# Random-feature attention on TensorE: key and query features as pairs of 64-row products, context product with its sides exchanged

## The chip, the cores and the metric

The kernel runs on one core of one Trainium2 chip. The metric is device time in microseconds from one launch. Five engines work side by side: TensorE (PE, with its weight loads as PEld), VectorE (DVE), ScalarE (ACT), GpSimd (POOL) and SyncE (SP), which issues most DMAs. TensorE reads on-chip memory (SBUF) and writes the eight PSUM banks of 128 partitions by 512 float32. All data here is float32, and each float32 product of the source becomes two weight loads and two passes on TensorE (a transpose is one of each).

## The reference, cut to what matters

The program is a layer of a network on 1250 nodes of width 512. It adds a graph convolution with two relations (two rounds), an attention block of depth 2, and a product-key memory with gathered rows. The change lies in the attention block. With 8 heads of 64 and 256 random features, each of its two layers computes (g and b left out):

```
def softmax_kernel(data, proj, is_query, eps=0.0001):
    normalizer = d ** (-0.25)
    data_dash = einsum('bhnd,md->bhnm', data * normalizer, proj)
    diag = sum(data ** 2, -1, keepdims=True) * 0.5 * normalizer ** 2
    m = max over features (query) or over nodes and features (key)
    return ratio * (exp(data_dash - diag - m) + eps)
q, k, v = y @ Wq + bq, y @ Wk + bk, y @ Wv + bv        # 8 heads of 64
qp, kp = softmax_kernel(q, proj, True), softmax_kernel(k, proj, False)
ctx = einsum('bhnm,bhnd->bhmd', kp, v);  k_sum = kp.sum(nodes)
o = einsum('bhmd,bhnm,bhn->bhnd', ctx, qp, 1 / (qp @ k_sum))
x = x + o @ Wo + bo;  then layer norm, MLP with gelu
```

## The kernel before, in words

The 1250 nodes are 10 tiles of 125 (`P`); the q, k, v products work on 5 pairs of tiles (`PAIRS`). There are no tiles chosen by a planner: each engine has its own hand-written list of instructions, in order, and semaphores in `m[...]` join them. `l` is the attention layer. Layer 0 runs from about 28 us to 380 us, then the MLP (to 668 us) and the two rounds of the graph convolution (to 1263 us), then attention layer 1 (to 1598 us), then the memory, with the MLP of layer 1 in it, to the end.

**Projection.** `projbd` (128 x 512) is a block-diagonal matrix: rows 0 to 63 hold the scaled projection in columns 0 to 255, rows 64 to 127 in columns 256 to 511, and the rest is zero. One product of k or q (128 rows = two heads) with it gives the features of two heads, 512 columns, in one bank. `attn1_dve` makes it at lines 460 to 464 by two zeroings and two scaled copies, ahead of the first norm (L483).

**Keys (`attn1_*`).** For each pair of tiles i, PE does the products for q, k, v (L570, L577, L584), the sums of squares in four 32-column groups (L590), and then 8 units n (tile j = n // 4, two heads c = n % 4), each one product at L610 into bank 4 + n % 4. Before unit 2 stand four transposes of the sums (L605), before unit 4 the 8 transposes of the next pair's normed rows (`turn(i + 1)`, L559). DVE takes the maximum of each unit (L514), ACT then copies the unit to `kdash` (L642), and this frees the bank: unit n waits for the copy of unit n - 4. DVE after unit 1: `spread` (L489) and the next norm (L483), for which `turn` waits. ACT after the copy of unit 3: `scale(i + 1)` (L623), for which the next q products wait. In layer 0 DVE has other work in its list too: 160 comparisons for the graph's edges (L356), 32 of them among the units of the first pair, the others among the k products, and the edge indices (L364 to L372), after unit 3 in pairs 1 to 4. A short chain of small steps over DVE and PE (L524 to L533) then forms the shift over all keys.

**Context (`attn2_*`).** ACT takes the exponentials (L656), DVE adds eps (L668), and PE multiplies for 10 tiles and 8 heads (L678): stationary `v_aug` (125 x 65: values and a column of ones), moving `kdash` (125 x 256), result 65 x 512 for two heads in one of banks 0 to 3. DVE and ACT copy these to `ctx_t` (L671, L661); in `attn3_pe` 16 transposes (L805) and four more copies (L723, L758) bring them to `ctx_sb`, 128 features by 65.

**Queries (`attn3_*`).** 40 units n (tile T, two heads c) go through a software pipeline on all three engines. In step n PE does the feature product of unit n (L800, banks 6, 7, 0, 1), the four transposes of unit n - 2 (L818), and the four output products of unit n - 3 (L829, 8 passes with 125 x 65); once per four steps also `out_turn` (L784) and `out_mm` (L792, 8 passes of 512 columns). DVE in step n: maximum (L715), bias (L717), copy with eps of unit n - 2 (L727), every second step a normalisation (L700, L702), every fourth, where n % 4 is 2, the residual (L707, L709) for n from 10. ACT: two exponentials (L749), and the copy L762. The transposes of units u with u % 4 = 1 write the bank that the residual reads, so they wait for L707 (line 814). SP's loads of the MLP's weights wait for `ctx`, and the loads of the graph's bases (L439) for the last residual. POOL scatters the edges in layer 0 (L284) in its own time, and then adds the two copies of the adjacency by DMA (L291).

## Time and profile before

| | us |
|---|---|
| median of 3 runs | 2761.16 |
| lowest, highest | 2752.94, 2769.96 |
| profiled execution, span from first to last instruction | 2754.8 |
| profiled execution, own time beyond its span | not given |
| PE busy | 2409.9 |
| DVE busy | 1468.9 |
| ACT busy | 681.1 |
| POOL busy | 1036.3 |

"Busy" is the time in which an engine executes; a PE product's end is modelled and lies some 0.16 us behind the start of the next, so the distance between starts is the better measure of its price. All steps below are taken from the profiled execution; L numbers are lines of the kernel.

### The profile page before, as it was taken

The numbers are of one execution on the slowest core, as the hardware profiler recorded it, in microseconds if no ns is written. First come the engines' busy times: TensorE is split into PE (matmuls) and PEld (weight loads), VectorE is DVE, ScalarE is ACT, GpSimd is POOL, SyncE is SP. The second block draws the span as 40 slices with busy tenths as digits, with TensorE's granted clock in tenths as the row PEclk, the third lists the DMA queues.
The fourth block names the chain that finished last, engine by engine and source line by source line (L and its number), as shares of the span: only waits on it lengthen the run. The fifth ranks groups of instructions, "written<-read, shape, count | busy, mean of one in ns | idle before, by whom it ended". The sixth has DMA issues, their size and how long they took to land.

```text
span 2754.8 us, 27581 instructions
## 1 busy us (share of the span) xinstructions
PE 2409.9 (87%) x9500; PEld 1234.4 (45%) x9500; DVE 1468.9 (53%) x3793; ACT 681.1 (25%) x1687; POOL 1036.3 (38%) x885
## 2 busy tenths in 40 slices
PE   3999989997999999999999987889879879875665
PEld 2656656665444444445656654433333333331210
DVE  3765675455666300002345614477677677677664
ACT  1346231211110011002364211223322332321222
POOL 0066877760111000000000000566666656666665
PEclk9999999998999999999999998999999999987856
DMA  9934145478466601440005000799999989989998
GB/s 304 297 64 127 2 109 117 98 157 223 160 181 196 154 1 52 108 112 19 1 1 172 1 8 8 267 327 342 337 327 342 335 316 348 333 317 340 341 358 313
DMA packets 235969, 524.42 MB, mean 190 GB/s; under 512 B 99362, under 2 KB 99737, under 8 KB 231675
## 3 DMA queue, kind: packets, MB, share of 16 engines
q0 software_dynamic: 170032, 379.99, 42.2%
q1 hardware_dynamic: 57477, 137.07, 16.2%
q10 hardware_dynamic: 8330, 5.71, 0.7%
q8 instruction: 71, 1.16, 0.2%
q14 instruction: 59, 0.48, 0.1%
HBM read 489.51 MB, written 45.34 MB: 194 GB/s over the span
## 4 chain that ended last, share of the span: by engine, by line
PE 67%; DVE 13%; DMA 8%; issue 5%; POOL 3%; another core or an unknown queue 2%; ACT 1%; SPq 0%; DVEq 0%; POOLq 0%; ACTq 0%
PE bank L1070 12%; PE bank L1325 6%; PE bank L1047 5%; PE bank L905 4%; PE bank L916 4%; PE bank L1305 4%; PE bank L1315 3%; PE bank L1259 3%; PE bank L678 3%; PE bank L792 3%; PE bank L570 3%; PE bank L584 2%; PE bank L1057 2%; PE bank L577 2%; DMA qv<-in_L_ffn_rows,qv 2%
## 5 line engine op out<-in xcount | busy, mean ns | idle before, releaser
L1228 POOL DMA_INDIRECT qv<-in_L_ffn_rows,qv x356 | 360.1, 1012 | 1009.4 <-issue 909.0
L1448 ACT ACTIVATE stage<-stage,qv 128x32 f32<-128x32 f32 x640 | 200.3, 321 | 576.8 <-issue 199.0
L1325 PE MATMUL bank<-qv,stage 128*32 128x512 f32 x712 | 257.6, 699 | 91.6 <-ACT stage L1448 48.4
L1612 DVE SCALAR_TENSOR_TENSOR qv<-qv,wreg 128x512 f32<-128x512 f32 x356 | 262.8, 746 | 118.2 <-DMA qv<-in_L_ffn_rows,qv 98.0
L284 POOL DMA_INDIRECT adj<-e_cnt,e_idx x80 | 163.7, 2046 | 193.7 <-issue 176.4
L284 POOL DMA_INDIRECT adj_b<-e_cnt,e_idx x80 | 167.3, 2091 | 62.5 <-issue 35.3
L1305 PE MATMUL bank<-stage,big 128*128 128x250 f32 x640 | 174.2, 399 | 7.5 <-ACT stage L1407 7.5
L1228 POOL DMA_INDIRECT big<-in_L_ffn_rows,qv x142 | 145.8, 1027 | 88.1 <-PE bank L1325 40.5
L1315 PE MATMUL bank<-big 128*125 128x512 f32 x320 | 173.0, 633 | 2.1 <-issue 2.1
L1070 PE MATMUL bank<-big,wreg 125*125 125x512 f32 x400 | 172.0, 592 | 0.0
L1070 PE MATMUL bank<-big,qv 125*125 125x512 f32 x400 | 171.8, 592 | 0.0
L1325 PE MATMUL bank<-big,stage 128*32 128x512 f32 x284 | 135.1, 722 | 35.9 <-ACT stage L1448 21.0
L1305 PEld LDWEIGHTS bank<-stage,big 128*128 128x128 f32 x640 | 115.6, 194 | 108.0 <-issue 91.1
L878 DVE SCALAR_TENSOR_TENSOR qv<-wreg,att_b,qv 128x2048 f32<-128x2048 f32 x60 | 138.4, 2348 | 32.9 <-DMA wreg<-in_L_gnn_basis 30.3
L1047 PE MATMUL bank<-qv,stage 128*125 128x512 f32 x320 | 148.1, 607 | 0.0
L1131 DVE TENSOR_TENSOR big<-bank,big 125x512 f32<-125x512 f32 x20 | 13.8, 692 | 247.2 <-PE bank L1070 247.2
L905 PE MATMUL bank<-stage,big 128*128 128x250 f32 x640 | 138.8, 377 | 1.2 <-ACT stage L937 1.2
L916 PE MATMUL bank<-big 128*125 128x512 f32 x320 | 139.0, 592 | 0.0
L1612 DVE SCALAR_TENSOR_TENSOR big<-big,qv,wreg 128x512 f32<-128x512 f32 x142 | 105.4, 746 | 55.0 <-DMA big<-in_L_ffn_rows,qv 48.9
L905 PEld LDWEIGHTS bank<-stage,big 128*128 128x128 f32 x640 | 122.4, 192 | 20.1 <-issue 6.0
L1325 PEld LDWEIGHTS bank<-qv,stage 128*32 128x32 f32 x712 | 32.2, 115 | 213.3 <-ACT stage L1448 109.8
L1099 POOL DMA_DIRECT2D stage<-in_L_gnn_basis x45 | 35.8, 955 | 226.1 <-DVE qv L1111 226.1
(227 smaller groups left out, 3984.8 us busy)
## 6 DMA issues: line engine op xcount, KB each, us to landing
wreg<-in_L_gnn_basis SPq DMA_DIRECT2D x30, 1024.0 KB
stage<-in_L_gnn_basis POOLq DMA_DIRECT2D x45, 512.0 KB, 4.5
big<-in_L_mix_W SPq DMA_DIRECT2D x4, 4096.0 KB
adj<-adj_b POOLq DMA_DIRECT2D x9, 1328.1 KB, 37.5
adj<-wreg SPq DMA_DIRECT2D x5, 2187.5 KB
adj_b<-wreg SPq DMA_DIRECT2D x5, 2187.5 KB
wreg<-adj SPq DMA_DIRECT2D x10, 1093.8 KB
qv<-adj SPq DMA_DIRECT2D x10, 1093.8 KB
```

Of the source, the lines that this page charges most:

```text
L284: nc.gpsimd.indirect_dma_start(out=(adj, adj_b)[g % 2], out_offset=bass.IndirectOffsetOnAxis(ap=e_idx[:, g:g + 1], axis=0), in_=e_cnt[:, g ...
L878: nc.vector.scalar_tensor_tensor(wrel[:, 0, r, :], wreg[:, n % BRING, :], att_b[:, 0, ds(i * BLOCKS + (r * BASES + n), 1)], wrel[:, 0, r, ...
L905: mm = nc.tensor.matmul(psum[F1_BANKS[n % 4]][:, 0:PT], w1_sb[:, k, 128 * n:128 * n + 128], y_t[:, k, :], start=(k == 0), stop=(k == KC - 1))
L916: mm = nc.tensor.matmul(psum[5 + j][0:P, :], act_t[:, k % HH, P * j:P * j + P], w2_sb[:, k, :], start=(k == 0), stop=(k == HC - 1))
L1047: mm = nc.tensor.matmul(psum[2 + 3 * j + r][0:P, :], gx_t[:, j, P * k:P * k + P], wrel[:, gl, r, 512 * k:512 * k + 512], start=(k == 0), s ...
L1070: mm = nc.tensor.matmul(psum[AGG_BANKS[j]][0:P, :], slabs[gl][:, j, c, :], zrel[:, c, :], start=(c == 0), stop=(c == COLT - 1))
L1228: nc.gpsimd.indirect_dma_start(out=ring[place(t, s)], out_offset=None, in_=a["L0_ffn_rows"], in_offset=bass.IndirectOffsetOnAxis(ap=slots_ ...
L1305: mm = nc.tensor.matmul(psum[F_BANKS[n % 2]][:, 0:PT], w1_sb[:, k, 128 * n:128 * n + 128], y_t[:, k, :], start=(k == 0), stop=(k == KC - 1))
L1315: mm = nc.tensor.matmul(psum[5 + j][0:P, :], act_t[:, k % HH, P * j:P * j + P], w2_sb[:, k, :], start=(k == 0), stop=(k == HC - 1))
L1325: nc.tensor.matmul(psum[7][WIDE * g:WIDE * g + WIDE, :], wsel[:, s % DRING, :], ring[place(t, s)][:, DIM:ROW], start=(s < 4), stop=(s >= S ...
L1448: nc.scalar.activation(wsel[:, s % DRING, :], mask, ACT.Relu, scale=inner[:, s:s + 1]).then_inc(p_diag, 1)
L1612: nc.vector.scalar_tensor_tensor(ring[place(t, s)][:, 0:DIM], ring[place(t, s)][:, 0:DIM], probs_of[t % 2][:, s:s + 1], xrep[:, s % 4, :], ...
```

## The change

The projection is kept once, as 128 rows by 256 columns (both halves alike). A step with two units n and n + 1 now does four products of 64 rows and 256 columns: heads in rows 0 to 63 (s = 0) go to one bank, heads in rows 64 to 127 (s = 1) to the next. So the units of a pair come from the same two 128-row blocks, and each bank holds the two heads of one s. Waits cover both banks. In the context product `kdash` is stationary (125 x 128, two halves per head) and `v_aug` moving (65 columns), which writes the layout of `ctx_sb` at once; `ctx_t`, its transposes and second copies are gone. `heads_of` picks the heads of a unit in the small tables of maxima and sums.

```diff
+        proj_t = projbd[:, 0:FEATS]
...
+        def heads_of(ap, u, s):
+            return ap.rearrange("p (u e s) -> p u e s", u=2, e=2)[:, u, :, s]
+        def two(ap):
+            return ap.rearrange("p (e m) -> p e m", e=2)
@@ -457,11 +464,7 @@
 
         def attn1_dve(dve, l):
             dve.wait_ge(m["pjT"], l * ADDS["pjT"] + 1)
-            for s in range(2):
-                rows = slice(64 * s, 64 * s + 64)
-                nc.vector.memset(projbd[rows, FEATS * (1 - s):FEATS * (2 - s)], 0.0).then_inc(m["pjS"], 1)
-                nc.vector.tensor_scalar(projbd[rows, FEATS * s:FEATS * s + FEATS], psum[7][rows, 0:FEATS], NORM, None,
-                                        ALU.mult).then_inc(m["pjS"], 1)
+            nc.vector.tensor_scalar(proj_t, psum[7][:, 0:FEATS], NORM, None, ALU.mult).then_inc(m["pjS"], 1)
             if l == 1:
                 dve.wait_ge(g_sem[1]["z"], 2 * TILES)
             else:
...
                     norm1(2 * i + 3)
                 for n in range(8):
-                    j, c = n // 4, n % 4
+                    j, u, s = n // 4, n % 4 // 2, n % 2
                     if l == 0 and i == 0 and n < 7:
                         merge_dve(dve, i, 4 * n + 4 * (n > 0), 4 + 4 * (n == 0))
                     dve.wait_ge(m["kd_pe"], l * ADDS["kd_pe"] + i * 8 + n + 1)
-                    nc.vector.tensor_reduce(kmax[:, 2 * i + j, 2 * c:2 * c + 2], psum[KD_BANKS[n % 4]][0:P, :].rearrange("p (s m) -> p s m", s=2),
+                    nc.vector.tensor_reduce(heads_of(kmax[:, 2 * i + j, :], u, s), two(psum[KD_BANKS[n % 4]][0:P, :]),
                                             AX, ALU.max).then_inc(m["kmx"], 1)
                     if n == 1:
...
                         mm = nc.tensor.matmul(psum[0][32 * c:32 * c + 32, PT * s:PT * s + PT], headsel[:, :], sq[:, s, c, :], start=True, stop=True,
                                               skip_group_check=True)
                 mm.then_inc(m["dg_mm"], 1)
-                for n in range(8):
-                    j, c = n // 4, n % 4
-                    if n < 2:
-                        pe.wait_ge(m["k"], l * ADDS["k"] + i * KC + KC + 1 + n)
-                    elif n < 4:
-                        pe.wait_ge(m["v"], l * ADDS["v"] + i * 2 + n - 1)
+                for n in range(0, 8, 2):
+                    j, u = n // 4, n % 4 // 2
+                    if n == 0:
+                        pe.wait_ge(m["k"], l * ADDS["k"] + i * KC + KC + 2)
+                    elif n == 2:
+                        pe.wait_ge(m["v"], l * ADDS["v"] + i * 2 + 2)
                     else:
-                        pe.wait_ge(m["kd"], l * ADDS["kd"] + i * 8 + n + 1)
+                        pe.wait_ge(m["kd"], l * ADDS["kd"] + i * 8 + n + 2)
...
                         turn(i + 1)
-                    nc.tensor.matmul(psum[KD_BANKS[n % 4]][0:P, :], k_t[:, c, P * j:P * j + P], projbd[:, :], start=True, stop=True).then_inc(m["kd_pe"], 1)
+                    for e in range(2):
+                        for s in range(2):
+                            rows = slice(64 * s, 64 * s + 64)
+                            mm = nc.tensor.matmul(psum[KD_BANKS[n % 4 + s]][0:P, FEATS * e:FEATS * e + FEATS], k_t[rows, 2 * u + e, P * j:P * j + P], proj_t[rows, :],
+                                                  start=True, stop=True, skip_group_check=True)
+                            if e == 1:
+                                mm.then_inc(m["kd_pe"], 1)
 
             pe.wait_ge(m["gmx"], l * ADDS["gmx"] + 1)
...
                 for n in range(8):
-                    j, c = n // 4, n % 4
+                    j, u, s = n // 4, n % 4 // 2, n % 2
                     if l == 1 and i == 2 and n == 0:
                         act.wait_ge(g_sem[1]["st"], 16 * PAIRS)
                     act.wait_ge(m["kmx"], l * ADDS["kmx"] + i * 8 + n + 1)
-                    nc.scalar.activation(kdash[:, 2 * i + j, 512 * c:512 * c + 512], psum[KD_BANKS[n % 4]][0:P, :],
-                                         ACT.Copy).then_inc(m["kd"], 1)
+                    nc.scalar.activation(kdash[:, 2 * i + j, :].rearrange("p (u e s m) -> p u e s m", u=2, e=2, s=2)[:, u, :, s, :],
+                                         two(psum[KD_BANKS[n % 4]][0:P, :]), ACT.Copy).then_inc(m["kd"], 1)
                     if n == 3 and i < PAIRS - 1:
                         scale(i + 1)
 
 
...
                         op.then_inc(m["kx"], 1)
+            if l == 0:
+                act.wait_ge(s_idx, 4 * PAIRS)
             for b in (1, 3):
                 act.wait_ge(m["ctx_pe"], l * ADDS["ctx_pe"] + b + 1)
-                nc.scalar.activation(ctx_t[:, 512 * b:512 * b + 512], psum[b][0:HD + 1, :], ACT.Copy).then_inc(m["cTa"], 1)
+                to, got = context_out(b)
+                nc.scalar.activation(to, got, ACT.Copy).then_inc(m["ctx"], 1)
 
         def attn2_dve(dve, l):
             for t in range(TILES):
@@ -668,16 +681,18 @@
                     nc.vector.tensor_scalar(kt, kt, EPS_K, None, ALU.add).then_inc(m["kf"], 1)
             for b in (0, 2):
                 dve.wait_ge(m["ctx_pe"], l * ADDS["ctx_pe"] + b + 1)
-                nc.vector.tensor_copy(ctx_t[:, 512 * b:512 * b + 512], psum[b][0:HD + 1, :]).then_inc(m["cT"], 1)
+                to, got = context_out(b)
+                nc.vector.tensor_copy(to, got).then_inc(m["ctx"], 1)
 
         def attn2_pe(pe, l):
             for t in range(TILES):
                 for hh in range(HEADS):
                     if hh % 4 == 0:
                         pe.wait_ge(m["kf"], l * ADDS["kf"] + 2 * t + hh // 4 + 1)
-                    mm = nc.tensor.matmul(psum[hh // 2][0:HD + 1, FEATS * (hh % 2):FEATS * (hh % 2) + FEATS],
-                                          v_aug[:, t, hh, :], kdash[:, t, FEATS * hh:FEATS * hh + FEATS],
-                                          start=(t == 0 and hh % 2 == 0), stop=(t == TILES - 1), skip_group_check=True)
+                    for q in range(2):
+                        mm = nc.tensor.matmul(psum[hh // 2][:, (HD + 1) * (2 * (hh % 2) + q):(HD + 1) * (2 * (hh % 2) + q + 1)],
+                                              kdash[:, t, FEATS * hh + 128 * q:FEATS * hh + 128 * q + 128], v_aug[:, t, hh, :],
+                                              start=(t == 0 and hh % 2 == 0 and q == 0), stop=(t == TILES - 1), skip_group_check=True)
                     if t == TILES - 1 and hh % 2:
                         mm.then_inc(m["ctx_pe"], 1)
...
                     dve.wait_ge(m["qd_pe"], l * ADDS["qd_pe"] + n + 1)
-                    nc.vector.tensor_reduce(qmax[:, n % 4, :], psum[QD_BANKS[n % 4]][0:P, :].rearrange("p (s m) -> p s m", s=2), AX, ALU.max).then_inc(m["qm"], 1)
+                    nc.vector.tensor_reduce(qmax[:, n % 4, :], two(psum[QD_BANKS[n % 4]][0:P, :]), AX, ALU.max).then_inc(m["qm"], 1)
                     dve.wait_ge(m["qm"], l * ADDS["qm"] + n + 1)
-                    nc.vector.scalar_tensor_tensor(qneg[:, n % 4, :], qmax[:, n % 4, :], -1.0, diag[:, T, 0, 2 * c:2 * c + 2],
+                    nc.vector.scalar_tensor_tensor(qneg[:, n % 4, :], qmax[:, n % 4, :], -1.0, heads_of(diag[:, T, 0, :], c // 2, c % 2),
                                                    ALU.mult, ALU.subtract).then_inc(m["qn"], 1)
-                if n == 1:
-                    for b in (0, 2):
-                        dve.wait_ge(m["cT_pe"], l * ADDS["cT_pe"] + b + 1)
-                        to, got = context_out(b)
-                        nc.vector.tensor_copy(to, got).then_inc(m["ctx"], 1)
                 if 2 <= n < UNITS + 2:
                     u = n - 2
                     dve.wait_ge(m["qT_pe"], l * ADDS["qT_pe"] + u + 5)
...
                     op.then_inc(m["qx"], 1)
-                if n == 1:
-                    if l == 0:
-                        act.wait_ge(s_idx, 4 * PAIRS)
-                    for b in (1, 3):
-                        act.wait_ge(m["cT_pe"], l * ADDS["cT_pe"] + b + 1)
-                        to, got = context_out(b)
...
             for n in range(UNITS + 6):
-                if n < UNITS:
-                    T, c = n // KC, n % KC
-                    pe.wait_ge(m["qx"], l * ADDS["qx"] + n + 1)
-                    nc.tensor.matmul(psum[QD_BANKS[n % 4]][0:P, :], q_t[:, c, P * T:P * T + P], projbd[:, :], start=True, stop=True).then_inc(m["qd_pe"], 1)
-                if n == 1:
-                    for b in range(4):
-                        pe.wait_ge(m["cTa" if b % 2 else "cT"], l * ADDS["cT"] + b // 2 + 1)
-                        for u in range(4):
-                            mm = nc.tensor.transpose(psum[T_BANKS[b]][:, (HD + 1) * u:(HD + 1) * (u + 1)], ctx_t[:, 512 * b + 128 * u:512 * b + 128 * u + 128],
-                                                     ident[0:HD + 1, 0:HD + 1])
-                        mm.then_inc(m["cT_pe"], 1)
+                if n == 2:
+                    pe.wait_ge(m["ctx"], l * ADDS["ctx"] + 4)
+                if n < UNITS and n % 2 == 0:
+                    T, u = n // KC, n % KC // 2
+                    pe.wait_ge(m["qx"], l * ADDS["qx"] + n + 2)
+                    for e in range(2):
+                        for s in range(2):
+                            rows = slice(64 * s, 64 * s + 64)
+                            mm = nc.tensor.matmul(psum[QD_BANKS[n % 4 + s]][0:P, FEATS * e:FEATS * e + FEATS], q_t[rows, 2 * u + e, P * T:P * T + P], proj_t[rows, :],
+                                                  start=True, stop=True, skip_group_check=True)
+                            if e == 1:
+                                mm.then_inc(m["qd_pe"], 1)
                 if 2 <= n < UNITS + 2:
                     u = n - 2
-                    if u < 2:
-                        pe.wait_ge(m["ctx"], l * ADDS["ctx"] + 4)
                     pe.wait_ge(m["qx"], l * ADDS["qx"] + u + 5)
                     if u % KC == 1 and u >= 9:
...
                         pe.wait_ge(m["o"], l * ADDS["o"] + 2 * T + 1 + c // 2)
-                    for s in range(2):
-                        hh = 2 * c + s
+                    for e in range(2):
+                        hh = 4 * (c // 2) + 2 * e + c % 2
                         for q in range(2):
                             mm = nc.tensor.matmul(psum[4 + hh // 4][0:P, (HD + 1) * (hh % 4):(HD + 1) * (hh % 4 + 1)],
-                                                  qfeat_t[:, v % 2, P * (2 * s + q):P * (2 * s + q) + P], ctx_sb[:, 2 * hh + q, :],
+                                                  qfeat_t[:, v % 2, P * (2 * e + q):P * (2 * e + q) + P], ctx_sb[:, 2 * hh + q, :],
                                                   start=(q == 0), stop=(q == 1), skip_group_check=True)
                     if c % 2:
                         mm.then_inc(m["o_pe"], 1)
```

## Rows read from the trace of the kernel before

**Rows 1.** The page: busy time by engine
```profile
PE 2409.9 (87%) x9500; PEld 1234.4 (45%) x9500; DVE 1468.9 (53%) x3793; ACT 681.1 (25%) x1687; POOL 1036.3 (38%) x885
```

**Rows 2.** Stretches: length; PE, PEld, DVE, ACT, POOL busy; PE clock; DMA share; GB/s
```profile
1425.30:1461.40 36.10, 36.09 (x161) 22.88 (x162) 14.56 (x21) 30.15 (x76) 0.00 (x0) 0.96 0.00 1
1479.00:1584.00 105.00, 99.77 (x537) 65.45 (x535) 67.22 (x157) 30.63 (x72) 0.00 (x0) 1.00 0.22 68
```

**Rows 3.** Groups by line: context product, maximum of the query features
```profile
L678 PE MATMUL bank<-big,qv 125*65 125x256 f32 x320 | 73.7, 395 | 6.0 <-DVE big L668 6.0
...
L715 DVE TENSOR_REDUCE small<-bank 125x2 f32<-125x512 f32 x80 | 55.1, 689 | 79.6 <-PE bank L800 79.0
```

**Rows 4.** Timeline of PE in the memory stage: a product of 64-row pairs
```profile
1990.66 0.80 PE L1305 MATMUL bank<-stage,big 128*128 128x250 f32 x3
1991.39 0.70 PE L1273 MATMUL bank<-wreg,qv 64*125 64x256 f32 x4
1992.02 0.69 PE L1315 MATMUL bank<-big 128*125 128x512 f32 x1
```

**Rows 5.** Timeline of the key units of one pair, layer 1
```profile
1293.46 1.98 PE L610 MATMUL bank<-projbd,stage 128*125 128x512 f32 x4
...
1294.62 0.69 DVE L514 TENSOR_REDUCE small<-bank 125x2 f32<-125x512 f32 x1 [0.89 <-PE bank L610]
...
1295.35 0.60 ACT L642 ACTIVATE big<-bank 125x512 f32<-125x512 f32 x1 [1.16 <-DVE small L514]
...
1296.25 0.54 DVE L483 TENSOR_SCALAR stage<-h,mv,rs 125x512 f32<-125x512 f32 x1
...
1298.85 1.90 ACT L623 ACTIVATE stage<-bank,cols 128x250 f32<-128x250 f32 x4
...
1301.72 1.85 PE L570 MATMUL bank<-stage,wreg 128*128 128x250 f32 x8
```

**Rows 6.** Timeline of one query step with n % 4 = 2, layer 1
```profile
1511.70 1.02 PE L800 MATMUL bank<-projbd,qv 128*125 128x512 f32 x2
...
1512.56 0.59 PE L818 MATMUL bank<-ident,big 125*128 125x125 f32 x4
...
1512.76 0.69 DVE L715 TENSOR_REDUCE small<-bank 125x2 f32<-125x512 f32 x1 [4.04 <-PE bank L800]
1512.89 0.95 PEld L829 LDWEIGHTS bank<-ctx_flat,stage 128*125 128x125 f32 x8
1512.99 0.99 PE L829 MATMUL bank<-ctx_flat,stage 128*125 128x65 f32 x8
...
1513.81 1.07 PE L800 MATMUL bank<-projbd,qv 128*125 128x512 f32 x2
...
1514.70 0.68 DVE L707 TENSOR_TENSOR h<-bank,h 125x512 f32<-125x512 f32 x1
...
1515.53 0.62 PE L818 MATMUL bank<-ident,big 125*128 125x125 f32 x4 [0.64 <-DVE h L707]
```

**Rows 7.** Timeline from the last context pass to the first query transposes, layer 0
```profile
241.55 1.88 PE L800 MATMUL bank<-projbd,qv 128*125 128x512 f32 x4
...
243.27 1.02 PEld L805 LDWEIGHTS bank<-ident,stage 65*128 65x128 f32 x15 [0.29 <-issue]
...
245.83 0.65 PE L818 MATMUL bank<-ident,big 125*128 125x125 f32 x4 [0.50 <-ACT ctx_flat L758]
```

**Rows 8.** Timeline of DVE at the start of layer 1
```profile
1263.90 0.27 DVE L462 MEMSET projbd<- 64x256 f32 x1
...
1265.41 0.46 DVE L483 TENSOR_SCALAR stage<-h,mv,rs 125x512 f32<-125x512 f32 x1
```

**Rows 9.** Busy time and clock by stretch (columns as in rows 2), end of layer 0
```profile
370.20:373.60 3.40, 1.73 (x13) 1.26 (x11) 2.15 (x5) 0.21 (x1) 3.10 (x2) 1.00 0.23 1
373.60:377.00 3.40, 2.97 (x4) 1.41 (x5) 0.63 (x2) 3.40 (x2) 2.79 (x3) 0.50 0.16 3
```

**Rows 10.** Chain of work that ended last, between the MLP and the graph convolution
```profile
629.56 39.30 DMA wreg<-in_L_gnn_basis
```

13 lines of the change are left out of this document (5 added, 8 removed).

## Prediction

> **What bounds the kernel now.** I read the page first, then busy time by stretch, groups by line, and the timeline of each part that the change touches. The page gives PE 87% of the span and no other engine more than 53% [rows 1]. In layer 1 PE is busy for 36.09 of 36.1 us in the context product and for 99.77 of 105 us in the queries [rows 2]; DVE waits 79.0 us for the query product [rows 3]. So PE sets the pace, and a shorter PE list pays only as far as the other engines' chains let it. Two of these are near. In the query steps with n % 4 = 2 PE already idles 0.64 us for the residual L707 [rows 6]. In the key part the next q products need `scale(i + 1)`, which ends at 1298.85 + 1.90 = 1300.75, only 0.97 us ahead of their start at 1301.72 [rows 5].
>
> **Price of the products.** Before, a unit of 512 columns takes 1512.56 - 1511.70 = 0.86 us, two passes of 0.43 [rows 6]. Right after an output product it takes 0.05 more (1.07 against 1.02, rows 6), because 65 columns don't cover the next weight load. The new form has a near relative in the memory stage [rows 4]: three passes of 250 columns, 0.21 each, end at 1990.66 + 0.64 = 1991.30; the 64-row block is recorded from 1991.39; the next 128-row product is recorded at 1992.02, with 0.69 instead of the usual 0.59 us, so its columns flow from 1992.12. Four passes of 256 columns thus cost 0.82 us: 0.43 for two streams side by side, and 0.39 for leaving and entering the 128-row form (0.09 of draining and 0.10 of bare weight load, twice). A new block has eight passes: 4 x 0.213 + 0.39 = 1.24 us for two units that cost 1.72 (1.82 behind output products). Two blocks in a row pay the switch once.
>
> The Trainium skill ("TensorEngine Tiling (Array Packing)", Key Properties) says that changing the tiling mode drains the engine. That speaks against this change: all query blocks stand alone between 128-row work. By that rule no block is free of the switch; the trace agrees and prices it at the 0.39 just read.
>
> **Projection.** Two zeroings and two copies run from 1263.90 until the norm at 1265.41, for which PE waits [rows 8]. One copy remains, about 0.4 plus 0.1 of hand-over; 1.0 us goes. In layer 0 the same four stand in the same DVE chain. Together -2.0.
>
> **Keys.** Zero is the record of the first unit, 1293.46 [rows 5]. New times: block 0 streams 0.10 to 0.96. DVE needs 0.20 more (rows 6: units end 1512.56, L715 starts 1512.76) and 0.69 per maximum, 0.61 back to back: unit 0 1.16 to 1.85, unit 1 to 2.46. ACT copies unit 1 to 3.09 (0.03 behind it, 0.60 long). The norm starts 0.08 behind unit 1's maximum (1294.62 + 0.86 + 0.69 = 1296.17 against 1296.25) and ends at 3.08. PE has done the four transposes of the sums and block 2 by 2.64, and must wait for this norm: a new stall of 0.6. `turn` 3.21 to 4.07, block 4 to 5.12, block 6 to 5.97. DVE takes units 2 and 3 to 4.30, ACT copies unit 3 until 4.93, `scale` (1.90) ends at 6.73, and q flows at 6.92. PE's list alone would be ready at 6.17; before it was 8.26. So 1.34 us per pair instead of 2.1: the wait that is late next is ACT's `scale`. The last pair has neither `turn` nor `scale`; its last maximum starts 1.0 earlier by the same count. Layer 1: 4 x 1.34 + 1.0 = 6.4. In layer 0 the first pair's units are paced by DVE with its edge comparisons, gain 0; three pairs 4.0; the last 0.5, since the edge indices stand in DVE's list before its last four maxima. Keys together -10.9.
>
> **Context.** 160 passes of 256 columns per layer, by columns half of 0.43, 0.2145 each, 34.3 us (the group's 73.7 us for both layers hold some half clock, rows 3). They become 320 passes with 128-column loads and 65 moving columns. The trace has this kind nearly: the output product's eight loads of 125 columns start over 0.95 - 0.19 = 0.76 us, 0.109 apart [rows 6], twice what 65 columns would stream. For 128 columns I take 0.112: 35.7 us, a loss of 1.4 per layer, +2.8. From below, the transposes' 128-column loads come (1.02 - 0.14) / 14 = 0.063 apart [rows 7]; that would be 20.1 us, a gain of 14 per layer. I stay at 0.112, because the 0.109 row is also a two-pass product. ACT with 30.15 us of work in this stretch [rows 2] keeps up.
>
> The Trainium skill ("TensorE: Matmul & The Clock Gate", Weight-path perf modes) says that fast weight load is not used for FP32 operands. By this the 0.063 is out of reach for a product and the 0.109 row is the right one; the transposes' row shows that some float32 loads do run faster.
>
> **Edits at nothing.** The maxima, copies and biases keep their sizes and only step over other heads; the wait for both banks is in the times above; ACT's moved wait for the edge indices in layer 0 is met long before the context ends. The MLP's weight loads start with `ctx`, some 2 us earlier, and nothing reads them for over 100 us.
>
> **Turn-around.** From the last context pass to the first query transposes it is 245.83 - 241.55 = 4.28 us, ended by the second copies L758 [rows 7]. New: switch and block 0 to 1.05, block 2 to 1.90 (the direct copies are ready before), maximum 1.25 to 1.94, bias, two exponentials (0.85), transposes at 3.1. Half a microsecond of later waits on unit 1 is made up by the unit that PE is ahead. -1.5 per layer, -3.0.
>
> **Queries.** Units 4 to 9: two units cost 2 x (0.91 + 0.43 + 0.82) = 4.32 before [rows 6], 3.74 after for n % 4 = 2; for n = 4 another 0.4 is lost waiting for L727. With 0.5 at n = 8 this is 1.3. From n = 10, steps with n % 4 = 2: zero is 1511.70; before, the transposes wait until 3.83 [rows 6]. The wait hangs on the first unit's maximum, which started at 1.06 and now starts at 1.25; so they start at 4.04, PE idle 1.5 instead of 0.86 (the second unit no longer fills this gap), and the half period is 0.2 longer. The other half (block, two times transposes and output product, `out_turn`, `out_mm`) is bound by PE and saves 1.77 - 1.24 = 0.53. Net 0.33 in each of 7 periods, -0.2 for the last: 2.1. Queries together -(1.3 + 2.1) x 2 = -6.8.
>
> **Sum.** -2.0 - 10.9 + 2.8 - 3.0 - 6.8 = -19.9 us, on the span of 2754.8: 2734.9. The median of the runs lies 6.4 above that span, within their spread, so I forecast 2761.2 - 19.9 = 2741.3. This asks that layer 0's share (9.3) comes through the MLP: there the last loads of the bases, 39.30 us on the chain [rows 10], share the DMAs with POOL's adding of the adjacencies. They start when DVE frees a buffer, so I let them move with it.
>
> **Rivals.**
> A, the chains give way (ACT's `scale` or the residual come earlier than I count) and PE's list decides. All of it would be 2.1 for each of 10 key pairs, 21 against my 10.9, and 0.53 for each of 36 query blocks, 19 against 6.8: 22 more, 2719. Half of it, which is what I mean by A: 2730. For it: PE's share [rows 1]; against it: the idle time already in rows 6 and the small slack in rows 5.
> B, slower: the clock falls in the context product. Its passes would stream 0.054 of every 0.112 us for 36 us on end. At the end of layer 0 PE is busy 1.73 of 3.4 us, and the next stretch has 0.50 of the full clock, 1.2 instead of 2.4 GHz; four passes of 512 columns fill 2.97 us there, not 4 x 0.43 [rows 9]. At that level a context pass costs twice, up to 36 us more per layer: 2741 + 72 = 2813. Against it: there PE also stood idle, here it never does. From about 20 us at half clock on, it outweighs the whole gain.
> C, the two row halves don't overlap, since a block has four products over two banks where rows 4 has two. A block then costs 0.85 more. By PE's list a key pair takes 1.3 more than before (nine pairs, 12), the second half of a query period 0.3 more (5), the first half 0.6 more by the later maximum (10); the other terms cancel: 2761 + 27 = 2788.
> D, layer 0's share is lost because the bases' loads end at a fixed time, set by the adjacency traffic: 2751.
>
> **Chances.** Forecast (2733 to 2749) 0.58, A 0.16, B 0.09, C 0.07, D 0.10. The range is 2720 to 2768; beyond it lie B and C, the far end of A and a fast weight load. A measurement of this kernel tells about 1% (27.6 us) from no change. Faster by more (below 2733.6) takes A or the low edge of the forecast: 0.27. Slower by more is B and half of C: 0.12. Within: 0.61.
>
> **What would show it.** Right: L610 and L800 blocks whose four passes of one row half come 0.21 apart with a partner beside each; L559 waiting 0.6 for L483 in the key part; the first L570 of a pair 6.9 us behind the first unit, ended by ACT L623; L678's successor with starts 0.11 apart and the stretch near 37 us; L818 waiting 1.5 for L707. Wrong: passes of a block one after the other (C), a clock below 0.9 in the context stretch (B), no wait of L559 (A), an MLP that ends earlier while the graph convolution doesn't (D).

## The result, and the profile after

The changed kernel takes 2828.45 us (median of 4 runs, 2809.09 to 2835.95), the kernel before 2761.32 beside it: ratio 1.023, interval 1.019 to 1.027. It is slower by 67 us, where 20 us of gain were forecast. The profiled execution has a span of 2834.1.

Busy time and clock by stretch, kernel before. The bounds are the starts of the stages' first PE instructions: keys of layer 0, its global maximum of the keys, context product, queries, then the MLP, then the four parts of layer 1, then the memory stage. The graph convolution and two parts of layer 1 are left out here (`...`; the two are shown with E5 and in rows 2). Columns as in rows 2.

```profile
28.40:200.00 171.60, 152.85 (x623) 100.29 (x623) 107.21 (x488) 60.92 (x126) 37.26 (x19) 1.00 0.75 231
200.00:204.20 4.20, 0.62 (x3) 0.34 (x3) 1.60 (x5) 2.66 (x8) 3.33 (x3) 0.85 0.20 1
204.20:241.60 37.40, 37.35 (x161) 23.43 (x162) 15.41 (x21) 30.18 (x76) 31.08 (x16) 0.93 0.17 2
241.60:387.10 145.50, 129.71 (x698) 84.95 (x696) 92.67 (x223) 46.99 (x95) 106.11 (x54) 0.98 0.35 72
387.10:681.70 294.60, 280.03 (x1001) 187.27 (x1001) 161.25 (x98) 52.05 (x104) 165.59 (x85) 0.97 0.67 157
...
1263.30:1421.00 157.70, 152.23 (x622) 100.59 (x622) 51.55 (x97) 59.57 (x125) 0.00 (x0) 0.98 0.01 4
...
1461.40:1599.10 137.70, 128.26 (x697) 84.35 (x695) 86.98 (x202) 39.99 (x93) 0.00 (x0) 1.00 0.26 87
1599.10:2754.80 1155.70, 911.40 (x4016) 362.30 (x4016) 738.65 (x2390) 312.65 (x900) 650.19 (x640) 0.88 0.82 296
```

The same view of the changed kernel:

```profile
28.20:195.00 166.80, 144.16 (x703) 102.26 (x703) 104.42 (x486) 60.32 (x126) 21.84 (x11) 0.98 0.76 237
195.00:199.70 4.70, 0.61 (x3) 0.33 (x3) 2.09 (x5) 3.16 (x9) 4.03 (x3) 0.69 0.18 1
199.70:268.20 68.50, 68.48 (x322) 68.36 (x322) 14.90 (x21) 29.46 (x74) 56.35 (x29) 0.50 0.18 2
268.20:428.60 160.40, 138.70 (x762) 101.98 (x761) 92.80 (x220) 46.84 (x93) 119.26 (x61) 0.84 0.33 64
428.60:714.50 285.90, 280.06 (x1000) 187.27 (x1001) 159.16 (x94) 52.14 (x104) 143.01 (x73) 0.98 0.66 162
...
1295.40:1445.50 150.10, 140.51 (x702) 100.11 (x702) 48.10 (x94) 58.68 (x125) 0.00 (x0) 0.98 0.01 4
1445.50:1450.00 4.50, 0.85 (x3) 0.57 (x3) 1.60 (x5) 4.04 (x9) 0.00 (x0) 0.56 0.00 0
1450.00:1518.50 68.50, 68.48 (x322) 68.36 (x322) 14.04 (x21) 29.94 (x76) 0.00 (x0) 0.50 0.00 1
1518.50:1668.30 149.80, 133.54 (x762) 98.06 (x762) 87.17 (x199) 39.77 (x91) 0.00 (x0) 0.88 0.24 80
1668.30:2834.10 1165.80, 919.54 (x4016) 366.44 (x4016) 738.97 (x2390) 313.31 (x900) 646.59 (x640) 0.87 0.81 293
```

The keys became shorter (171.6 to 166.8, 157.7 to 150.1). The context product became 31.1 and 32.4 us longer [rows 2 for layer 1 before], at a granted clock of 0.50, which is 1.2 GHz, from its first to its last instruction. The queries became 14.9 and 12.1 longer at 0.84 and 0.88. Two smaller parts belong to the sum: MLP -8.7, memory stage +10.1, where the change touches nothing. In the MLP's stretch PE arrives at the graph convolution 41.5 us later than before and then waits 4.59 us for the features instead of 13.32 (lines under E13 and E14), which is the 8.7. The memory stage's stretch lies between 1147 and 1176 us in the seventeen profiled executions of this study, and follows none of the edits; I attribute nothing to it. All parts together (with -0.7 in the graph convolution and +0.7 in the global maxima) give the 79.3 us, to 0.2, by which the two profiled spans differ; the medians differ by 67.

The groups that answer to [rows 3]:

```profile
L693 PE MATMUL bank<-qv,big 125*128 125x65 f32 x640 | 137.1, 418 | 6.5 <-DVE big L681 6.5
...
L727 DVE TENSOR_REDUCE small<-bank 125x2 f32<-125x512 f32 x80 | 54.8, 685 | 94.5 <-PE bank L805 94.5
```

137.1 us for 640 passes is 0.214 a pass, nearly twice the 0.112 of the forecast. DVE's maxima cost what they did (685 against 689 ns); they wait 94.5 instead of 79.0 us for PE.

The timeline of PE in one key pair of layer 1, which answers to [rows 5]:

```profile
1324.61 1.13 PE L616 MATMUL bank<-projbd,stage 64*125 64x256 f32 x8
...
1327.78 1.05 PE L562 MATMUL bank<-ident,stage 125*128 125x125 f32 x8 [0.34 <-ACT big L651]
1328.76 2.00 PE L616 MATMUL bank<-projbd,stage 64*125 64x256 f32 x16
1331.36 0.90 PE L573 MATMUL bank<-stage,wreg 128*128 128x250 f32 x3 [0.61 <-ACT stage L632]
```

Here the forecast's steps stand: a block of eight passes is 1.13 us of records (the two row halves run side by side); the transposes of `turn` wait 0.34 us (forecast 0.6), which the profile puts down to ACT's copy of unit 1, and that copy ends within 0.01 us of the norm L486, as the forecast had it (3.09 and 3.08); and the next q product comes 6.75 us behind the first unit's record, ended by ACT's `scale`; forecast was 6.92, before it was 8.26.

### The profile page after: what moved, and what is told of

It is laid out like the page before. It is cut to its first block, busy times and chain, and to the rows that moved or that the text cites. A ratio compares the mean times of both kernels' runs of the same rounds, so it can differ in the third digit from the quotient of the medians.

```text
span 2834.1 us, 28783 instructions
## 1 busy us (share of the span) xinstructions
PE 2475.0 (87%) x10108; PEld 1361.2 (48%) x10108; DVE 1463.0 (52%) x3783; ACT 679.7 (24%) x1683; POOL 1034.0 (36%) x885
## 4 chain that ended last, share of the span: by engine, by line
PE 66%; DVE 14%; DMA 9%; issue 4%; POOL 3%; ACT 2%; another core or an unknown queue 1%; SPq 0%; DVEq 0%; POOLq 0%; ACTq 0%
PE bank L1069 12%; PE bank L1324 6%; PE bank L1046 5%; PE bank L693 5%; PE bank L1304 4%; PE bank L1314 3%; PE bank L904 3%; DMA qv<-in_L_ffn_rows,qv 3%; PE bank L915 3%; PE bank L1258 3%; PE bank L573 3%; PE bank L792 3%; PE bank L580 2%; PE bank L587 2%; PE bank L1056 2%
## 5 line engine op out<-in xcount | busy, mean ns | idle before, releaser
L1324 PE MATMUL bank<-qv,stage 128*32 128x512 f32 x712 | 266.6, 715 | 93.6 <-ACT stage L1447 59.4
L284 POOL DMA_INDIRECT adj_b<-e_cnt,e_idx x80 | 164.1, 2051 | 58.5 <-issue 23.8
L1304 PEld LDWEIGHTS bank<-stage,big 128*128 128x128 f32 x640 | 117.7, 198 | 111.4 <-issue 93.9
L877 DVE SCALAR_TENSOR_TENSOR qv<-wreg,att_b,qv 128x2048 f32<-128x2048 f32 x60 | 138.4, 2347 | 47.9 <-DMA wreg<-in_L_gnn_basis 45.6
L693 PE MATMUL bank<-qv,big 125*128 125x65 f32 x640 | 137.1, 418 | 6.5 <-DVE big L681 6.5
L693 PEld LDWEIGHTS bank<-qv,big 125*128 125x128 f32 x640 | 136.7, 333 | 6.7 <-DVE big L681 6.7
```

The source lines that it names most:

```text
L284: nc.gpsimd.indirect_dma_start(out=(adj, adj_b)[g % 2], out_offset=bass.IndirectOffsetOnAxis(ap=e_idx[:, g:g + 1], axis=0), in_=e_cnt[:, g ...
L693: mm = nc.tensor.matmul(psum[hh // 2][:, (HD + 1) * (2 * (hh % 2) + q):(HD + 1) * (2 * (hh % 2) + q + 1)], kdash[:, t, FEATS * hh + 128 * ...
L1304: mm = nc.tensor.matmul(psum[F_BANKS[n % 2]][:, 0:PT], w1_sb[:, k, 128 * n:128 * n + 128], y_t[:, k, :], start=(k == 0), stop=(k == KC - 1))
L1324: nc.tensor.matmul(psum[7][WIDE * g:WIDE * g + WIDE, :], wsel[:, s % DRING, :], ring[place(t, s)][:, DIM:ROW], start=(s < 4), stop=(s >= S ...
```

## The experiments

E1 to E4 take the change apart, E5, E6 and E15 look into the context product, E7 and E8 into the queries, E9 to E12 put parts together, and E13 and E14 test where layer 0's gain goes. The kernel before, run beside them, took 2770.91 us for E1 to E4, 2771.57 for E5 to E8, 2759.36 for E9 to E12 and 2764.79 for E13 to E15, so totals are to be compared by their ratio to it, given with its 95% interval.

**E1, the context alone.** The kernel before with only the context's edits; the product's new lines are:

```diff
+                    for q in range(2):
+                        mm = nc.tensor.matmul(psum[hh // 2][:, (HD + 1) * (2 * (hh % 2) + q):(HD + 1) * (2 * (hh % 2) + q + 1)],
+                                              kdash[:, t, FEATS * hh + 128 * q:FEATS * hh + 128 * q + 128], v_aug[:, t, hh, :],
...
```

> The kernel before with only the context product exchanged. Theory 1 (each part acts through its own stretch): the exchanged product alone keeps TensorE at half its clock for the whole context stretch, granted clock 0.50, 68 us instead of 37 per layer; the direct copies give back 1 to 2 us; about 2761 + 62 - 3 = 2820, and the query stretches keep a clock of 0.98 or more and their 138 to 146 us. Rival (knock-on): the query stretches run at 0.84 to 0.88 because the context left the engine slow; then they show it here as well, 12 to 15 us longer each, about 2845.

2820.68 us, ratio 1.017 (1.011 to 1.022). Windows of the context and the queries, both layers:

```profile
205.50:273.80 68.30, 68.30 (x321) 68.30 (x321) 15.46 (x21) 29.85 (x75) 56.16 (x29) 0.50 0.18 2
273.80:418.80 145.00, 130.36 (x682) 84.75 (x682) 91.16 (x220) 46.24 (x93) 106.53 (x54) 0.97 0.34 70
1451.40:1519.70 68.30, 68.30 (x321) 68.30 (x321) 14.05 (x21) 29.80 (x75) 0.00 (x0) 0.50 0.00 1
1519.70:1659.00 139.30, 130.30 (x682) 84.72 (x682) 86.34 (x199) 39.24 (x91) 0.00 (x0) 0.98 0.25 85
```

The exchanged product alone carries the loss of the context, with nothing else of the change in the kernel. The two stretches lose 63 us; 5.5 of them come back before the graph convolution starts, and the total, 50 us by the medians, agrees with that within its interval (30 to 61 us). The queries behind it run as before, so their loss has a cause of its own.

**E2, the pairs alone.** The changed kernel with the context of before (256 moving columns, `ctx_t` transposed).

> The changed kernel with the old context product, its transposes and second copies. Theory 1: the query part loses its clock by its own form (periods of 13.3 us with 1.4 us of idle engine and 64-row blocks), mean granted clock about 0.88 there, about +13 us per layer against keys and projection at -12 for both: about 2761 - 12 + 26 = 2775. Rival (knock-on): the clock of the query stretches is above 0.97 and they gain 2 to 4 us per layer: about 2743.

2782.29, ratio 1.0026 (1.0003 to 1.0049). Contexts 37.2 and 37.7 us at 0.93 and 0.92, keys 167.7 and 149.9, but queries of 157.4 and 153.1 at 0.86 and 0.87. The keys' gain is eaten by the queries, and their clock is low without the exchanged context.

**E3, pairs in the keys alone** (projection of before, its two diagonal blocks used).

> The kernel before with only the key features as 64-row pairs (from the block-diagonal matrix, so its making stays). Theory 1: 1.3 us less per pair of tiles as in the changed kernel, layer 1's key part 6.5 us shorter, layer 0's 4: about 2751 if layer 0's share comes through the MLP, 2755 if the loads of the bases take it back. Rival: the 64-row blocks cost clock here too (mean below 0.96 in 1269 to 1415) and nothing is gained: 2761.

2764.61, ratio 0.9969 (0.9947 to 0.9991): a gain of 6.3 us by the medians, 8.6 by the ratio. Keys 169.2 and 150.9, queries as before at 145.4 and 139.3.

**E4, pairs in the queries alone.**

> The kernel before with only the query features as 64-row pairs. Theory 1: half clock in a third of the query stretches, about +13 us per layer: 2787. Rival (knock-on from the context): clock above 0.97 and 2 to 4 us less per layer: 2755.

2792.24, ratio 1.0065 (1.0034 to 1.0097): a loss of 21 us by the medians, 18 by the ratio. Queries 149.1 at 0.92 and 156.3 at 0.85. The transposes' group in the queries of layer 1:

```profile
L831 PE MATMUL bank<-ident,big 125*128 125x125 f32 x160 | 30.1, 322 | 12.6 <-DVE h L714 11.4 <-ACT ctx_flat L765 1.0 <-DVE stage L734 0.3
```

PE idles 11.4 us for the residual in eight steps, 1.42 each, in either layer. That is the wait of 1.5 that the prediction named; what it did not follow is the clock.

**E5, context with the clock held.** E1 with four products of 512 columns (results overwritten) beside the short instructions of the global maximum, where PE had idled:

```diff
+            nc.tensor.matmul(psum[2][0:P, :], wreg[:, 2, 0:P], wreg[:, 2, 0:512], start=True, stop=True, skip_group_check=True)
             pe.wait_ge(m["gmx"], l * ADDS["gmx"] + 1)
...
+            for _ in range(3):
+                nc.tensor.matmul(psum[2][0:P, :], wreg[:, 2, 0:P], wreg[:, 2, 0:512], start=True, stop=True, skip_group_check=True)
```

> E1 with four products of 512 columns added on TensorE (into bank 2, unused results): one ahead of the wait for the maximum over all keys, three behind the last product of that chain, so that the engine works through most of the 4.3 us in which it idled and enters the context product at full clock. Theory 1a (the exchanged product itself lets the clock fall): full clock at the start of the context stretch, passes 0.11 apart there, then a fall to 0.50 within the stretch and 0.213 apart; the stretch is 60 us or more. Theory 1b (it only fails to bring the clock back after the idle chain): the clock stays at 1.00 and the stretch takes 36 us; the whole is about 2760. Rival (loads of 128 columns take 0.21 at any clock): 68 us at clock 1.00.

2766.85 in one run, 5 under the kernel before beside it, where E1 is 50 above. The context of both layers:

```profile
205.10:240.90 35.80, 35.80 (x321) 35.80 (x321) 14.47 (x21) 29.93 (x76) 30.81 (x16) 1.00 0.19 3
...
1430.30:1466.10 35.80, 35.80 (x321) 35.80 (x322) 14.03 (x21) 29.83 (x75) 0.00 (x0) 1.00 0.01 2
```

The same 320 passes at 2.4 GHz throughout: 0.112 each, the very price forecast (35.7 us). So the exchanged product does not make the clock fall. What differs is the level it is entered at. The kernel before and E1 enter their contexts alike; windows over the way in, first before, then E1:

```profile
1421.00:1425.30 4.30, 0.65 (x3) 0.37 (x3) 1.60 (x5) 4.04 (x9) 0.00 (x0) 0.96 0.00 0
1425.30:1428.30 3.00, 2.99 (x7) 1.70 (x8) 1.24 (x2) 3.00 (x9) 0.00 (x0) 0.50 0.00 0
1428.30:1461.40 33.10, 33.10 (x155) 21.18 (x154) 13.33 (x20) 27.15 (x68) 0.00 (x0) 1.00 0.00 1
```

```profile
1447.40:1451.40 4.00, 0.50 (x3) 0.41 (x3) 1.51 (x5) 3.82 (x8) 0.00 (x0) 0.93 0.00 0
1451.40:1459.70 8.30, 8.30 (x40) 8.30 (x40) 3.47 (x5) 8.30 (x22) 0.00 (x0) 0.50 0.01 3
1459.70:1519.70 60.00, 60.00 (x283) 60.00 (x282) 10.58 (x16) 21.50 (x54) 0.00 (x0) 0.50 0.00 1
```

In both, PE is nearly idle for the 4 us of the global maximum, the clock falls near the end of them, and it is at half when the context begins. The product with 256 moving columns has full clock after 3.0 us. The one with 65 is still at half after 68. In the changed kernel the clock falls earlier (0.69 and 0.56 over the same stretch, listed above), but that isn't what costs: in E3, layer 1, the clock is at 0.81 over the last 12.1 us ahead of the context and at 0.50 over its first 2.9, and the 256-column product still takes only 37.4 us.

**E6, a product of 512 columns in every tile** on top of E5.

> E5 with one more product of 512 columns (0.86 us, into bank 7, unused result) behind each of the first nine tiles of the context product, 7.7 us of added work per layer. If the clock answers to how much TensorE streams, it stays full and a stretch takes 35.7 + 7.7 = 43 to 45 us, shorter than without the added work. If it does not, the stretch is 68 + 15 = 83 us at half clock.

2782.62 in one run; contexts of 43.5 us at 1.00. Nine fillers cost 7.7 us, 0.86 each, and hold nothing that E5 did not hold already.

**E15, the clock brought back in mid product.** E1 with six products of 512 columns behind the fifth of the ten tiles:

```diff
                     if t == TILES - 1 and hh % 2:
                         mm.then_inc(m["ctx_pe"], 1)
+                if t == 4:
+                    for _ in range(6):
+                        nc.tensor.matmul(psum[7][0:P, :], wreg[:, 2, 0:P], wreg[:, 2, 0:512], start=True, stop=True, skip_group_check=True)
```

> The kernel of E1 (only the context's sides exchanged) with six products of 512 columns behind the fifth of the ten tiles of the context; their results are overwritten. If the exchanged product only fails to bring the clock back, it is at 0.50 up to the products and at 1.00 from there to the end of the context: five tiles of 6.8, about 8 us of products, five tiles of 3.6, 58 to 60 us in all, and 16 us below E1's time over both layers. If the exchanged product itself makes the clock fall, it falls again behind the products, and the context takes 68 us and 5 to 10 more.

2794.25 in one run, 29 above the kernel before beside it, where E1 is 50 above. The two contexts give 19.8 of this; 16 were forecast. Layer 0's context, before, in and behind the fillers:

```profile
205.10:239.10 34.00, 34.00 (x160) 34.00 (x161) 14.89 (x19) 29.10 (x73) 27.96 (x15) 0.50 0.17 2
239.10:245.40 6.30, 6.30 (x14) 2.84 (x14) 0.00 (x0) 0.00 (x0) 5.39 (x4) 0.83 0.19 1
245.40:263.30 17.90, 17.90 (x162) 17.89 (x161) 0.86 (x2) 0.39 (x1) 14.12 (x8) 1.00 0.17 2
```

160 passes at half take 34.0 us, the other 160 at full take 17.9, in one product, with PE recorded busy in every microsecond. The contexts are 58.3 and 58.5 us, the forecast was 58 to 60. E5 and E15 together settle it: in these stretches the product keeps whichever clock it meets. Whether its 65 columns do that or the 128-column load ahead of each pass, no run separates.

The Trainium skill ("TensorE: Matmul & The Clock Gate", Part 1: The HAM clock gate) says that the clock follows how busy the engine has been and that activity releases it. The rows above show that busy time by the record is not that activity: 68.30 of 68.30 us busy did not bring the clock back, 3.0 us of a 256-column product did. The measurement decides.

**E7, queries with the wait filled.** E4 with two products of 256 columns in the wait for the residual (results overwritten, as in E5):

```diff
+                if n % 4 == 3 and 11 <= n < UNITS:
+                    for _ in range(2):
+                        nc.tensor.matmul(psum[QD_BANKS[(n - 3) % 4]][0:P, 0:256], wreg[:, 3, 0:P], wreg[:, 3, 0:256], start=True, stop=True, skip_group_check=True)
```

> E4 with two products of 256 columns (0.86 us at full clock, into a free bank, unused results) put where the engine waits 1.4 us for the residual, in each of 8 steps per layer. Theory 2a (the longer idle piece makes the clock fall in the queries): the clock of the query stretches returns to 0.97 or more, they take 134 to 144 us, and the whole is 10 to 25 us faster than E4. Theory 2b (the 64-row products count for less, whatever stands in the idle piece): clock and time stay as in E4, about 2790.

2773.87, ratio 1.0004 (0.9979 to 1.003); E4 was at 1.0065. Queries of both layers:

```profile
241.60:382.90 141.30, 126.26 (x809) 90.28 (x808) 91.75 (x222) 47.52 (x95) 104.10 (x53) 0.98 0.35 72
...
1468.40:1602.50 134.10, 124.64 (x809) 89.67 (x809) 86.80 (x201) 40.51 (x93) 0.00 (x0) 1.00 0.26 89
```

With the clock at 0.98 and 1.00 the queries are 4.2 and 3.6 us shorter than before, near the forecast's 3.4 per layer. The loss in E4's query stretches is all clock. Yet the total only equals the kernel before. Layer 0's 4.2 us are lost ahead of the graph convolution: the MLP stretch is 11.7 us longer (306.3 against 294.6), and POOL's adding of the adjacency copies starts 10 us later in this execution (605.36 against 595.41; see E13). Layer 1's 3.6 us are less than the interval can show, and the memory stage, untouched, took 18 us longer in this execution.

**E8, the new order with full rows.** Both units' products of before at even n, with the same wait, and no 64-row form:

```diff
+                if n < UNITS and n % 2 == 0:
+                    pe.wait_ge(m["qx"], l * ADDS["qx"] + n + 2)
+                    for k in (n, n + 1):
...
```

> The kernel before with the order of the changed kernel for queries (both units of a pair at even steps, both banks awaited), but each unit still one 128-row product of 512 columns. Theory 2a (idle piece and order): the engine waits about 1.4 us for the residual here too, and the clock falls as in E4, query stretches 149 to 156 us, about 2785. Theory 2b (the rows): the clock stays at 0.97 or more and the stretches take 138 to 148 us, about 2770 with the runs of this chip.

2788.41, ratio 1.0049 (1.0023 to 1.0075). The queries of both layers, and the transposes of layer 0:

```profile
240.90:393.70 152.80, 131.32 (x697) 87.38 (x695) 94.98 (x223) 47.62 (x95) 112.42 (x57) 0.96 0.34 67
...
1466.40:1613.30 146.90, 131.30 (x698) 87.39 (x697) 89.90 (x201) 40.63 (x93) 0.00 (x0) 0.98 0.24 81
```

```profile
L819 PE MATMUL bank<-ident,big 125*128 125x125 f32 x160 | 24.0, 273 | 11.4 <-DVE h L707 11.4
```

Neither theory came whole: the time is that of the first, the clock nearly that of the second. PE idles as long for the residual (11.4 us), and the clock stays near full (0.96, 0.98 against E4's 0.92, 0.85; before had 0.98 and 1.00). So the gap alone takes little of the clock; with the 64-row blocks beside it, it takes more. The blocks are also shorter than the products that they replace (1.24 us forecast against 1.72), so PE has less work between the gaps; no run separates the form from that. The order costs 7 and 9 us in the two layers, 6.2 of it in each as PE's longer idle time before the transposes (11.4 against 5.2 us in the same group of before, 0.64 a step in [rows 6]); nothing shortens the products to pay for it.

**E9, the whole change with the fillers of E5 and E7.**

> The changed kernel, whole, with the fillers of E5 (four products of 512 columns around the chain over all keys) and of E7 (two of 256 columns in the wait for the residual). Theory (the clock is the only thing that went wrong): context 35.8 us at clock 1.00, queries about 141 and 135 us (the turn-around by direct copies 1 to 2 us less still), keys as in the changed kernel, 5 and 7.7 us less than before; about 22 us faster than before, ratio 0.992. Rival (the pairs of the key part lower the clock ahead of the fillers, as E2 and E3 show 0.50 right behind them): the context starts at half clock and stays there in one layer or both, 30 to 60 us slower than that.

2749.99 (12 runs) against 2759.36, ratio 0.9962 (0.9947 to 0.9978): faster than the kernel before by 9.4 us (10.5 by the ratio), where about 22 were expected, and faster than the changed one, which is slower than before by 2.3%. Attention's parts in its profile:

```profile
28.20:195.60 167.40, 142.97 (x705) 101.14 (x705) 105.22 (x488) 60.30 (x126) 31.55 (x16) 0.99 0.75 236
195.60:200.40 4.80, 3.42 (x9) 1.41 (x9) 2.15 (x5) 3.20 (x9) 4.18 (x3) 1.00 0.19 5
200.40:236.30 35.90, 35.87 (x320) 35.81 (x320) 14.94 (x21) 29.51 (x74) 29.89 (x16) 1.00 0.17 2
236.30:374.70 138.40, 123.48 (x793) 88.66 (x792) 91.12 (x220) 46.79 (x93) 101.91 (x51) 0.99 0.35 73
374.70:681.10 306.40, 280.72 (x1000) 187.72 (x1001) 166.86 (x126) 52.14 (x104) 181.62 (x91) 0.95 0.66 152
...
1262.70:1411.40 148.70, 140.15 (x704) 99.37 (x704) 48.05 (x94) 58.72 (x125) 0.00 (x0) 0.99 0.01 4
...
1451.60:1584.30 132.70, 123.44 (x793) 88.61 (x792) 86.13 (x199) 39.78 (x91) 0.00 (x0) 1.00 0.27 90
```

Against before, attention of layer 0 is 12.2 us shorter (167.4 + 4.8 + 35.9 + 138.4 = 346.5; before 171.6 + 4.2 + 37.4 + 145.5 = 358.7) and that of layer 1 14.2. But the MLP's stretch has grown by 11.8: the graph convolution starts at 681.1, before at 681.7. Layer 0's gain is gone by then.

**E10, the whole change with E5's fillers alone.**

> The changed kernel with the fillers of E5 alone. Theory: context 35.8 us at clock 1.00; the query stretches keep their losses of E4 (3 to 18 us each) since nothing fills the residual's wait: about 2765 to 2775, 15 to 25 us slower than E9.

2768.59, ratio 1.0037 (1.0012 to 1.0061). Contexts 35.8 and 35.9 at 1.00, queries 157.5 and 147.3 at 0.85 and 0.90. Each filler restores its own stage only.

**E11, E9 with the context of before.**

> E9 with the old context product. Theory: its stretch takes 34.5 to 36 us at full clock, 1.4 less than the exchanged one by columns and loads, and the turn-around 1 to 2 us more: equal to E9 within 3 us, so the exchanged sides are worth nothing by themselves, about 0.992 of before.

2750.40, ratio 0.9965 (0.9941 to 0.9989), no different from E9. Contexts of 34.6 and 34.7 at 1.00 are 1.2 shorter than the exchanged ones; turn-around and queries are 3.4 and 3.0 longer (141.8 and 135.7 against 138.4 and 132.7). Those 4 us in the profile are below what the totals tell apart.

**E12, the kernel before with E5's fillers.**

> The kernel before with the fillers of E5 alone. Theory: the context stretches go from 37.3 and 36.1 to about 34.6 us each, 2 to 4 us less in all, which the runs can hardly tell from nothing: ratio 0.998 to 1.000. If the gain of E9 came from the fillers and not from the change, this run would show it: ratio 0.992.

2766.56, ratio 1.0020 (0.9998 to 1.0041). Its contexts run at 1.00 in 34.6 us, 2.8 and 1.5 less than before, and the total gains nothing. The fillers alone don't give E9's gain; with the pairs they do, whichever way the context's sides stand (E11).

**E13 and E14, fewer adding DMAs** in E9 and in the kernel before (nine tenths of the adding of the second adjacency copy are left out, and SP waits for the one DMA that is left):

```diff
-            for n in range(SUMS):
+            for n in range(1):
                 rows = slice(272 * n, min(272 * n + 272, CELLS // 1250))
                 nc.gpsimd.dma_start(adj_rows[rows, :], adj_b_rows[rows, :], accum_op=ALU.add, max_dma_last_dim=5000).then_inc(s_sum, 16)
```

> The kernel of E9 with only the first of the ten DMAs that add the second copy of the adjacency to the first; nine tenths of that adding are left out, so the graph convolution multiplies by half of most of its matrix. If layer 0's gain is held back by that adding (rival D: in nearly all runs the graph convolution starts 83 to 86 us after the adding starts, however long layer 0 took before it), then the load of the features behind it falls from 16.3 us to the 6.4 us of the kernel before or less, the start of the graph convolution moves from 681.1 us to 668 to 671, and the time is 10 to 13 us below that of E9: about 2738. If the adding has nothing to do with it, the start stays at 681 and the time within 3 us of E9.

> The kernel before with the same nine tenths of the adding left out. If the adding holds up the start of the graph convolution, the start moves here too, but by less, since layer 0 itself ends about 12 us later than in E13: from 681.7 to 672 to 678, so that E13 stands 20 to 27 us below this kernel, where E9 stood 9.4 us below the kernel before. If the adding has nothing to do with it, this kernel takes the time of the one before within 3 us.

E13 2717.87, E14 2739.54, on the same chip and beside the same runs of the kernel before (2764.79; ratios 0.9818, 0.9783 to 0.9853, and 0.9898, 0.9864 to 0.9933). The difference of the two is 21.7 us, forecast 20 to 27, where E9 stood 9.4 below the kernel before. E13's own time missed: it was to be 10 to 13 us below E9's, and it is 46.9 below the kernel before beside it, where E9 was 9.4 below. First, the start of the graph convolution in the kernel before and in E9, then in E13, then in E14, last in the changed kernel:

```profile
681.69 1.06 PE L1024 MATMUL bank<-ident,stage 125*128 125x125 f32 x4 [13.32 <-DMA stage<-xn_d]
```

```profile
681.13 1.07 PE L1029 MATMUL bank<-ident,stage 125*128 125x125 f32 x4 [24.45 <-DMA stage<-xn_d]
```

```profile
658.31 0.59 PE L1029 MATMUL bank<-ident,stage 125*128 125x125 f32 x4
```

```profile
668.48 0.59 PE L1024 MATMUL bank<-ident,stage 125*128 125x125 f32 x4
```

```profile
714.51 1.07 PE L1023 MATMUL bank<-ident,stage 125*128 125x125 f32 x4 [4.59 <-DMA stage<-xn_d]
```

With the adding, PE idles 13.3 us before and 24.5 in E9 for the features: E9's PE is ready 11.7 us earlier (656.7 against 668.4) and waits 11.1 longer. On the chain that ended last the same load takes

```profile
675.12 6.44 DMA stage<-xn_d
```

in the kernel before and

```profile
664.74 16.26 DMA stage<-xn_d
```

in E9; issued ten microseconds earlier, it lands at 681 in both. With nine tenths of the adding gone PE waits for nothing, and layer 0's gain stands at the start of the graph convolution, 10.2 us. Both starts moved further than I expected (668 to 671 and 672 to 678): the last loads of the bases, on the chain for about 40 us before and in E9, are off it too.

The adding doesn't start at the same time in every execution either: POOL reaches it when its scatter is done, at 595.41 us in the kernel before, 598.50 in E9 and 605.36 in E7. In the twelve profiled executions with all of the adding and without a context at half clock (before, E2 to E12), the graph convolution starts 82.6 to 89.0 us behind it.

## Why the prediction was wrong

The sign was wrong and the time lies outside the range. Point by point, by its own steps:

**The step that failed** is rival B's "Against it: there PE also stood idle, here it never does", and with it the sum, taken at full clock throughout. The price at half clock was right: up to 36 us per layer forecast, 32 measured. The mechanism was put the wrong way round. I asked whether the product would make the clock fall, and counted the idle time inside it. E5 and E15 show that it doesn't; it fails to bring it back. The fall happens ahead of it, while PE idles for the global maximum, and it stood in the trace of before: a clock of 0.96 over the context in [rows 2] is 3 us at half at its start, which the 256-column product repaired each time. I had even noted half-clock time in the group of [rows 3], and read it as a small correction to a price instead of asking what ended it. Of the 79.3 us between the two profiled spans, 63.5 arise here (31.1 + 32.4).

**Queries and turn-around.** Forecast -6.8 and -3.0, measured +27.0. The steps themselves hold: the transposes wait 1.42 us for the residual (forecast 1.5), and with the clock held E7's queries gain 4.2 and 3.6 (forecast 3.4 a layer), and those of E9, turn-around included, 7.1 and 5.0 (forecast 4.9). The failed step is the same one: the prediction lengthened a gap from 0.64 to 1.5 and put 64-row blocks beside it, and priced neither at the clock. E8 shows that the longer gap with full rows keeps 0.96 or more; E7, that the blocks with a filled gap keep 0.98 or more. What makes the two together cost so much no run here shows.

**Keys and projection.** Forecast -10.9 and -2.0, measured -12.4 together (4.8 in layer 0 and 7.6 in layer 1). E3, with the projection of before, gives the keys alone: 2.4 and 6.8, against 4.5 and 6.4. In layer 1 the projection's four instructions became one of 0.41 us. The count by hand-overs, down to the `scale` that the next q product waits for, was right; of layer 0's 4.5 only 2.4 came, and why is open.

**Context at full clock.** Forecast +1.4 per layer, measured +1.2 (35.8 in E5 against 34.6 in E12): the price of 0.112 a pass and its choice against the transposes' 0.063 were right.

**Rivals.** A didn't come: the waits in the key pair shown above stand where forecast. C is excluded by the blocks of 1.13 us. D is real, and hidden in the changed kernel, whose layer 0 ends too late for the adding to matter: there PE waits only 4.6 us for the features. It decides in E9, where it takes 11.6 of the 26 us, and E13 against E14 gives them back. My forecast let the bases' loads move with DVE; they and the features share the DMAs with the adding, which starts when POOL has scattered the edges, however early layer 0 ends.

With the clock held at both places the whole change brings 9.4 us (E9), near the 10.6 that the forecast's sum less D's 9.3 would leave. That nearness is partly luck: in the trace layer 1 is 14.2 us shorter, where its own terms in the forecast give 10.9. A version with the context of before does as well (E11).

**Slips in the working**, none of which moves the forecast's sum. Layer 0's terms add up to 9.0 and not to the 9.3 of the sum and of D. In the queries, PE's idle time before was 0.64 [rows 6], as the prediction says at its start, and not 0.86. In B, a loss of 20 us takes some 40 us spent at half clock, where the prediction writes 20: the 68.5 us at half are 32.7 more than the 35.8 of E5.

## What to carry to other kernels

Where a stretch's clock in the profile is a little under 1.00, look up where the half-clock time lies and which instruction ended it, before you replace that instruction: a cheap product may be what brings the clock back. Price every reshaped product at both levels of the clock, by the level that it will be entered at, and count as PE's idle time also what stands ahead of it. If a reshaped product is entered after a gap, a few wide products in the gap are worth a trial; here some 3 us of products per layer, in a gap, saved 32 us per layer (E5 against E1).

## What the runs showed that I had not expected

A product of 65 moving columns with a 128-column load in each pass held the half clock for 68 us with PE recorded busy all the time, and ran at full clock for 36 us when it met it (E5, E15). The same gap of 1.42 us costs little of the clock beside 128-row products (0.98 in layer 1, E8) and much beside 64-row blocks (0.85, E4). A DMA issued ten microseconds earlier may land at the same time while another queue is adding: 16.26 us in place of 6.44 for the same load.
